# Conv-attention hybrid on one core: angles counted in turns on VectorE, centred weights, a new order table

## The chip, the core and the metric

The kernel runs on one core of one Trainium2 chip. The metric is device time in microseconds of that core, the median of several runs. Engines are named as the profile names them: PE is TensorE, PEld its weight load, DVE is VectorE, ACT is ScalarE, POOL is GpSimd, SP is SyncE.

## The reference

The input is x, 8 x 16 x 16 x 128 in float32: 8 batches of 256 tokens with 128 channels. Three layers follow one another; everything but the first softmax and the layer norms works token by token or head by head.

```
o  = gamma * softmax(f g^T) @ hh @ Wv + bv + xf     # f, g, hh: 16-wide projections of xf, with biases
t  = o
y  = LN(t)
c  = cos(y + theta); p = cumprod(c) per head, p[0] = prod(c[1:])     # 8 heads of 16
z  = y + softmax(p p^T / 4) p @ W_comb.T + b_comb
x1 = LN(z) * ln1_g + ln1_b
q  = cos(x1[:, :8]) * cos(phi)
z2 = x1 + relu(q @ W1.T + b1) @ W2.T + b2
t  = t + LN(z2) * ln2_g + ln2_b
u  = LN(t); sel = sigmoid(u @ expert_sel.T), the best 2 of 32 experts kept as weights w
t  = t + sum over experts of w * (relu(u @ keys) @ values)
```

LN subtracts the mean over the 128 channels and divides by the standard deviation. The biases and norm gains hold real numbers, not zeros and ones.

## The kernel before

One batch is two tiles of 128 tokens (`TB = 2`), kept with tokens on the partitions as 128 x 2 x 128. Every batch goes through six chains of steps, and there are 8 batches (`NB`):

- **conv**: x is transposed and projected by one weight matrix `wproj` (f, g and the product Wh Wv), f and g are split into three bf16 parts and stacked on POOL (`FGp`), scores, exp (`EA`), transposed (`ETs`), and multiplied with `HW` into `conv_ps`. DVE writes `T0 = conv_ps * gden + XR` (L854), where `gden` (L847) is gamma over the softmax sum and `XR` is x plus a constant row.
- **proj**: layer norm of T0 (`bn_stats` L765, `bn_aggr` L769 on DVE; `rsqrt` as two instructions on POOL, L1063 and L1065; `Y` on DVE, L775), then the angle Y + theta + pi/2, brought into a range that the Sin table takes, then Sin, cumulated products (L894), `PA`, and the fp16 parts `LS` and `RS`.
- **attn**: transposes of LS and RS, copied by DVE to `LT` (L907) and `RT` (L912), 8 score matmuls (L509) with 8 exps (L707), context (L519), a turn, the combination with `wcT_sb` (L542), `Z` (L925).
- **ffn**: layer norm of Z with its gain and bias (`ffn_norm`), 8 cosines per token, hidden layer, output (L570), `Z2` (L958).
- **norm**: second layer norm into `T1`, third into `XTK` (L775).
- **moe**: selection of experts, 4 pairs of matmul groups (L621, L625, and L606 into `moe_ps`), and `OB = moe_ps + T1` (L1013), which SP stores.

The angle's range is reduced in six instructions. POOL's `proj_angle` adds theta (L1135), and its helper `reduce_angle` finds the nearest number of whole turns by adding and taking away a large constant (L1070, L1072); then it makes `YB = Y + b_comb` (L1141), which `attn_combine` adds later. DVE's `proj_reduce` takes the turns off in two steps (L877, L880) and clamps (L885). The ffn chain does the same on 128 x 16 elements: POOL L1173, L1070, L1072, then `X1B` (L1177), DVE L939, L942, L947. `norm_affine` on DVE makes X1 in two passes, (Z - mean) * gain into `ZN` (L783) while POOL makes rstd, then times rstd plus bias (L788).

Each engine has one stream of instructions and takes them in order. `run_steps` sorts all 344 steps (name, batch) by one number and calls, on each engine, that engine's part of every step in that order; an engine whose part waits for a semaphore stands there, with everything behind it. Before, the number is a start of the step in its chain plus a start of the chain for the batch:

```
for _, b, name in sorted((at + CHAIN[name.split("_")[0]][b], b, name)
                         for name, at in START.items() for b in range(NB)):
```

The first conv output is followed by weight transposes on PE, and DVE's `proj_norm` of batch 0 ends with two small setup instructions (L863, L865). ACT loads a table of functions whenever the next function is in another set than the last one: Exp, Sin.

Of the kernel before, what the change touches and what calls it, by code (L numbers as in the profile page):

```python
# [26 lines left out]

START = {  # L30
    "conv_transpose": 0.000, "conv_project": 0.131, "conv_stack": 0.478, "conv_scores": 0.664, "conv_turn": 0.991,
    "conv_output": 1.190,
    "proj_norm": 0.000, "proj_angle": 0.375, "proj_reduce": 0.557, "proj_cos": 0.794, "proj_split": 1.014,
# [11 lines left out]
CHAIN = {
    "conv": (0.000, 4.654, 5.883, 7.128, 8.599, 9.969, 11.330, 12.652),
    "proj": (4.213, 6.104, 7.449, 8.826, 10.191, 11.562, 12.928, 14.505),
    "attn": (5.828, 7.430, 8.902, 10.276, 11.607, 12.925, 14.284, 15.872),  # L50
    "ffn": (7.444, 8.943, 10.284, 11.705, 13.063, 14.512, 16.131, 17.455),
    "norm": (9.557, 10.883, 12.224, 14.018, 15.617, 16.569, 18.277, 19.630),
    "moe": (10.535, 11.888, 13.236, 14.828, 16.048, 17.547, 18.900, 20.600),
# [1188 lines left out]
```

## Time and profile before

| | us |
|---|---|
| median of 3 runs | 266.65 (266.59 to 267.42) |
| span of the profiled execution | 265.1 |
| PE busy | 193.9 (73%) |
| DVE busy | 174.5 (66%) |
| ACT busy | 132.0 (50%) |
| POOL busy | 126.3 (48%) |

The span reaches from the first to the last instruction of one profiled execution. Of that execution's own time the profile gives only this span; the runs' times hold some 1.5 us more (266.65 less 265.1), which lie around it. Busy shares are averages over the whole span.

### The profile page before, as it was taken

The numbers are of one execution on the slowest core, as the hardware profiler recorded it, in microseconds if no ns is written. First come the engines' busy times: TensorE is split into PE (matmuls) and PEld (weight loads), VectorE is DVE, ScalarE is ACT, GpSimd is POOL, SyncE is SP. The second block draws the span as 40 slices with busy tenths as digits, with TensorE's granted clock in tenths as the row PEclk, the third lists the DMA queues.
The fourth block names the chain that finished last, engine by engine and source line by source line (L and its number), as shares of the span: only waits on it lengthen the run. The fifth ranks groups of instructions, "written<-read, shape, count | busy, mean of one in ns | idle before, by whom it ended". The sixth has DMA issues, their size and how long they took to land.

```text
span 265.1 us, 4762 instructions
## 1 busy us (share of the span) xinstructions
PE 193.9 (73%) x1488; PEld 144.9 (55%) x1488; DVE 174.5 (66%) x580; ACT 132.0 (50%) x276; POOL 126.3 (48%) x321
## 2 busy tenths in 40 slices
PE   3372466649775667998899889859788868597395
PEld 2161253423662445786488668637666747476265
DVE  1333464776858788977888788698767566347323
ACT  2523537457458166646846673855447362412021
POOL 3706798265757568555744743376153161022100
PEclk9999999995979979999999999999999999979869
DMA  3385000000000000000000000000000000000000
GB/s 64 107 162 117 0 1 4 0 1 2 0 0 2 0 1 4 0 2 21 1 2 0 22 0 1 22 0 4 0 22 2 1 19 2 21 0 0 22 0 20
DMA packets 12624, 4.33 MB, mean 16 GB/s; under 512 B 6276, under 2 KB 12472, under 8 KB 12600
## 3 DMA queue, kind: packets, MB, share of 16 engines
q1 hardware_dynamic: 12104, 3.94, 6.4%
q8 instruction: 12, 0.20, 0.3%
q10 hardware_dynamic: 496, 0.09, 0.2%
q14 instruction: 12, 0.10, 0.1%
HBM read 2.98 MB, written 1.05 MB: 15 GB/s over the span
## 4 chain that ended last, share of the span: by engine, by line
PE 38%; DVE 29%; issue 10%; POOL 10%; ACT 9%; DMA 1%; ACTq 1%; POOLq 0%; DVEq 0%
PE hidden_ps L621 9%; PE moe_ps L606 6%; PE ffn_ps L570 4%; POOL rstd L1065 4%; DVE HWT L1007 3%; DVE RT L912 3%; DVE st L765 2%; PE sc_ps L509 2%; PE attn_ps L519 2%; PE hidden_ps L625 2%; PE conv_ps L476 2%; PE conv_ps L441 2%; ACT EB_ L707 1%; DMA bv_b<-in_L_conv_bv 1%; DVE ARG L877 1%
## 5 line engine op out<-in xcount | busy, mean ns | idle before, releaser
L707 ACT ACTIVATE EB_<-sc_ps 128x512 f32<-128x512 f32 x64 | 35.1, 597 | 15.1 <-PE sc_ps L509 14.3
L621 PE MATMUL hidden_ps<-XTT,keys_sb 128*128 128x256 f32 x128 | 40.8, 412 | 2.4 <-DVE HWT L1007 2.4
L747 ACT ACTIVATE HR<-hidden_ps 128x256 f32<-128x256 f32 x64 | 24.4, 384 | 35.7 <-PE hidden_ps L625 35.5
L606 PE MATMUL moe_ps<-val_sb,HWT 128*128 128x128 f32 x256 | 33.9, 277 | 2.6 <-DVE HWT L1007 2.6
L606 PEld LDWEIGHTS moe_ps<-val_sb,HWT 128*128 128x128 f32 x256 | 31.0, 192 | 6.6 <-DVE HWT L1007 3.5
L1007 DVE TENSOR_TENSOR HWT<-hidden_ps,HR 128x256 f32<-128x256 f32 x64 | 25.1, 418 | 12.1 <-ACT HR L747 10.3
L1063 POOL TENSOR_SCALAR var<-mv 128x2 f32<-128x2 f32 x32 | 6.6, 205 | 53.2 <-DVE mv L769 52.7
L509 PE MATMUL sc_ps<-RT,LT 128*128 128x256 f16 x128 | 22.9, 290 | 10.0 <-ACT EB_ L707 4.6
L621 PEld LDWEIGHTS hidden_ps<-XTT,keys_sb 128*128 128x128 f32 x128 | 20.6, 202 | 9.3 <-DVE HWT L1007 4.6
L1065 POOL TENSOR_TENSOR rstd<-var,minushalf 128x2 f32<-128x2 f32 x32 | 22.3, 697 | 2.7
L509 PEld LDWEIGHTS sc_ps<-RT,LT 128*128 128x128 f16 x128 | 10.7, 102 | 19.8 <-issue 13.6
L519 PE MATMUL attn_ps<-EB_,PA 128*32 128x256 f32 x256 | 18.1, 403 | 3.2 <-ACT EB_ L707 3.1
L570 PE MATMUL ffn_ps<-w2T_sb,HID 128*128 128x128 f32 x128 | 18.5, 306 | 2.3 <-ACT HID L730 2.3
L570 PEld LDWEIGHTS ffn_ps<-w2T_sb,HID 128*128 128x128 f32 x128 | 17.5, 219 | 3.0 <-ACT HID L730 2.9
L625 PE MATMUL hidden_ps<-WT,spread 96*128 96x256 f16 x64 | 18.1, 283 | 0.8 <-DVE WT L998 0.8
L730 ACT ACTIVATE HID<-ffn_ps 128x512 f32<-128x512 f32 x16 | 9.6, 598 | 8.9 <-PE ffn_ps L563 8.9
L683 ACT ACTIVATE EA<-conv_ps,nmx 128x256 f32<-128x256 f32 x16 | 7.4, 470 | 9.8 <-DVE nmx L836 9.7
L519 PEld LDWEIGHTS attn_ps<-EB_,PA 128*32 128x32 f32 x256 | 6.9, 113 | 9.8 <-ACT EB_ L707 5.6
L912 DVE COPY RT<-sc_ps 64x1024 f16<-64x1024 f16 x16 | 11.1, 694 | 0.3
L775 DVE TENSOR_SCALAR XTK<-T,mv,rstd 128x128 f32<-128x128 f32 x16 | 4.9, 345 | 9.2 <-POOL rstd L1065 9.2
L673 ACT COPY HW<-conv_ps 128x256 f32<-128x256 f32 x8 | 3.0, 372 | 16.0 <-DVE FGs L824 16.0
L476 PE MATMUL conv_ps<-HW,ETs 128*128 128x128 f32 x64 | 9.8, 300 | 1.4 <-DVE ETs L843 1.4
(174 smaller groups left out, 449.0 us busy)
## 6 DMA issues: line engine op xcount, KB each, us to landing
X<-in_x SPq DMA_DIRECT2D x8, 128.0 KB, 7.9
out<-OB SPq DMA_DIRECT2D x8, 128.0 KB, 1.8
keys_sb<-in_L_ffn_keys SPq DMA_DIRECT2D x1, 512.0 KB, 7.8
val_sb<-in_L_ffn_values SPq DMA_DIRECT2D x1, 512.0 KB, 9.0
w_sb<-in_L_attn_W SPq DMA_DIRECT2D x1, 256.0 KB, 2.8
g_b<-in_L_attn_ln_g SPq DMA_DIRECT2D x2, 64.0 KB, 5.5
be_b<-in_L_attn_ln_b SPq DMA_DIRECT2D x2, 64.0 KB, 6.5
bv_b<-in_L_conv_bv ACTq DMA_DIRECT2D x1, 64.0 KB, 3.6
```

Of the source, the lines that this page charges most:

```text
L476: last = mm(conv_ps[:, t * C:(t + 1) * C], ETs[:, b % 2, m, t * P:(t + 1) * P], HW[:, b % 2, m, :], start=(m == 0), stop=(m == TB - 1))
L509: last = mm(sc_ps[h % 2][:, t * N:(t + 1) * N], LT[:, h // 2, t * P:(t + 1) * P], RT[:, h % 2, h // 2, :], start=True, stop=True)
L519: last = mm(attn_ps[32 * j:32 * j + 32, g * N:(g + 1) * N], PA[:, b % 2, t, h, :], EB_[:, h, t, :], start=(t == 0), stop=(t == TB - 1))
L570: last = mm(ffn_ps[:, t * C:(t + 1) * C], HID[:, k, t * P:(t + 1) * P], w2T_sb[:, k, :], start=(k == 0), stop=(k == FB - 1))
L606: last = mm(moe_ps[:, t * C:(t + 1) * C], HWT[:, k % 4, t * P:(t + 1) * P], val_sb[:, k, :], start=(k == 0 and t == 0), stop=(k == EB - 1) ...
L621: mm(hidden_ps[i][:, 0:N], keys_sb[:, k * EPB:(k + 1) * EPB, :].rearrange("p e h -> p (e h)"), XTT[:, b % 2, :], start=True, stop=True)
L625: mm(hidden_ps[i][:, N:2 * N], spread[:, k, :], WT[:, b % 2, :], start=True, stop=True).then_inc(s_moe_ps, 1)
L707: fn(EB_[:, h, :, :].rearrange("p t n -> p (t n)"), sc_ps[h % 2][:, :], ACT.Exp, scale=1.0 / math.sqrt(DK)).then_inc(s_prob, 1)
L747: fn(HR[:, k % 4, :], hidden_ps[i][:, 0:N], ACT.Relu).then_inc(s_relu, 1)
L912: V.tensor_copy(RT[q, i, :, :].rearrange("p j n -> p (j n)"), b16(sc_ps[0], F16)[q, :]).then_inc(s_RT, 1)
L1007: V.tensor_tensor(HWT[:, k % 4, :], hidden_ps[i][:, N:2 * N], HR[:, k % 4, :], ALU.mult).then_inc(s_hw, 1)
L1065: G.tensor_tensor(rstd[:, which, b, :], var[:, which, b, :], minushalf[:, :], ALU.pow).then_inc(rs, 1)
```

## The change

What the diff does, part by part:

- **Turns.** `reduce_angle` and POOL's part of it are gone. DVE's `proj_reduce` now has all three steps: turns = Y/(2 pi) + (theta/(2 pi) + 1/4), the nearest whole number by adding `ROUND`, and the fraction, which ACT's Sin takes with scale -2 pi. `ffn_angle` does the same on 16 columns. Nothing is clamped. `ARG` and `QA` shrink from 6 parts to 3.
- **Centred weights.** At setup DVE takes from b_comb its mean and from each row of the transposed W_comb its mean (`center`, three instructions each), so that Z less its mean needs no subtraction. `ffn_norm` on DVE is then one pass, Z * rstd * gain; `ZN` is gone. ln1_b no longer enters X1: it is added with b2 (`b12_b`) on POOL, and for the 8 angle columns in `be1q_b`.
- **Gamma** goes into `wproj` when it is copied from PSUM, which now waits for `w_in`; `gden` is gone.
- **Order.** `START` and `CHAIN` are replaced by one table of ranks, of which two rows stand below.

```diff
-START = {
+ORDER = {
...
+    "attn_transpose": (15, 45, 80, 114, 154, 191, 235, 273),
...
+    "ffn_norm": (54, 74, 118, 160, 188, 223, 282, 304),
...
             dve.wait_ge(s_wv_ps, 1)
-            V.tensor_copy(wproj[:, 2 * D:2 * D + C], hidden_ps[1][:, 0:C]).then_inc(s_wproj_sb, 1)
             dve.wait_ge(w_in, W_LOADED)
+            V.tensor_scalar(wproj[:, 2 * D:2 * D + C], hidden_ps[1][:, 0:C], gam[:, 0:1], None, ALU.mult).then_inc(s_wproj_sb, 1)
...
-                dve.wait_ge(s_crden, b + 1)
-                V.tensor_scalar(gden[:, b, :], rden[:, b, :], gam[:, 0:1], None, ALU.mult).then_inc(s_cgain, 1)
...
+            def center(dst, src, mean, summed, done):
+
+                V.tensor_reduce(mean[:, 0:1], src[:, :], AX.X, ALU.add).then_inc(summed, 1)
+                dve.wait_ge(summed, 1)
+                V.tensor_scalar(mean[:, 1:2], mean[:, 0:1], 1.0 / C, None, ALU.mult).then_inc(summed, 1)
+                dve.wait_ge(summed, 2)
+                V.tensor_scalar(dst[:, :], src[:, :], mean[:, 1:2], None, ALU.subtract).then_inc(done, 1)
...
-                    V.tensor_scalar(theta2[:, :], theta_b[:, :], math.pi / 2, None, ALU.add).then_inc(s_theta2, 1)
+                    V.tensor_scalar(theta2[:, :], theta_b[:, :], TURN, 0.25, ALU.mult, ALU.add).then_inc(s_theta2, 1)
+                    V.tensor_scalar(be1q_b[:, :], be1_b[:, 0:NQ], TURN, 0.25, ALU.mult, ALU.add).then_inc(s_be1q, 1)
+                    V.tensor_tensor(b12_b[:, :], be1_b[:, :], b2_b[:, :], ALU.add).then_inc(s_b12, 1)
+                    center(bcc_b, bc_b, bc_mean, s_bc_mean, s_bc)
+                    dve.wait_ge(s_wcT, 1)
+                    center(wcT_sb, wc_raw, wc_mean, s_wc_mean, s_wc)
...
             def proj_reduce(b):
-                dve.wait_ge(s_y_k, b + 1)
...
+                V.scalar_tensor_tensor(out=A[:, 0].rearrange("p t (h d) -> p (t h) d", d=DK),
+                                       in0=Y[:, b % 2].rearrange("p t (h d) -> p (t h) d", d=DK), scalar=TURN,
+                                       in1=theta2[:, None, :].to_broadcast([P, TB * H, DK]),
+                                       op0=ALU.mult, op1=ALU.add).then_inc(s_y_turns, 1)
+                dve.wait_ge(s_y_turns, b + 1)
+                V.tensor_scalar(A[:, 1], A[:, 0], ROUND, None, ALU.add).then_inc(s_y_near, 1)
+                dve.wait_ge(s_y_near, b + 1)
...
+                V.scalar_tensor_tensor(out=A[:, 2], in0=A[:, 1], scalar=ROUND, in1=A[:, 0],
+                                       op0=ALU.subtract, op1=ALU.subtract).then_inc(s_y_frac, 1)
...
-                norm_affine(b, X1[:, b % 2], ZN[:, b % 2], Z[:, b % 2], 1, s_z_mv, s_z_rstd, g1_b[:, :],
-                            [be1_b[:, :]] * TB, s_z_n, s_x1)
+                dve.wait_ge(s_z_rstd, b + 1)
+                for t in range(TB):
+                    last = V.scalar_tensor_tensor(out=X1[:, b % 2, t, :], in0=Z[:, b % 2, t, :], scalar=rstd[:, 1, b, t:t + 1],
+                                                  in1=g1_b[:, :], op0=ALU.mult, op1=ALU.mult)
+                last.then_inc(s_x1, 1)
...
-            def reduce_angle(b, A, a, k1, k):
...
-                G.tensor_tensor(ARG[:, b % 2, 0].rearrange("p t (h d) -> p (t h) d", d=DK),
...
-                reduce_angle(b, ARG[:, b % 2], s_y_arg, s_y_k1, s_y_k)
```

How the order moves, at the three places that the prediction speaks of. The first is DVE in the end of batch 0's `proj_norm` and its angle. Before (L865 is theta, L824 is batch 1's projection with its bias, L894 the cumulated product):

```order
L865 TENSOR_SCALAR theta<-theta_b 128x16
L775 TENSOR_SCALAR Y<-T,mv,rstd 128x128 x2
L877 SCALAR_TENSOR_TENSOR ARG<-ARG 128x256
L880 SCALAR_TENSOR_TENSOR ARG<-ARG 128x256
L885 TENSOR_SCALAR ARG<-ARG 128x256
L824 TENSOR_TENSOR FGs<-conv_ps,bfg 128x64
L894 SCALAR_TENSOR_TENSOR SC<-scanmask,CS 128x256
```

Now:

```order
L891 TENSOR_SCALAR theta<-theta_b 128x16
L892 TENSOR_SCALAR be1q_b<-be_b 128x8
L893 TENSOR_TENSOR b_b<-be_b,b_b 128x128
L878 TENSOR_REDUCE bc_mean<-bc_b 128x1
L880 TENSOR_SCALAR bc_mean<-bc_mean 128x1
L882 TENSOR_SCALAR bcc_b<-bc_b,bc_mean 128x128
L878 TENSOR_REDUCE wc_mean<-wc_raw 128x1
L880 TENSOR_SCALAR wc_mean<-wc_mean 128x1
L882 TENSOR_SCALAR wcT_sb<-wc_raw,wc_mean 128x128
L844 TENSOR_TENSOR FGs<-conv_ps,bfg 128x64
L795 TENSOR_SCALAR Y<-T,mv,rstd 128x128 x2
L909 SCALAR_TENSOR_TENSOR ARG<-Y,theta 128x256
L914 TENSOR_SCALAR ARG<-ARG 128x256
L918 SCALAR_TENSOR_TENSOR ARG<-ARG 128x256
L928 SCALAR_TENSOR_TENSOR SC<-scanmask,CS 128x256
```

Eight setup rows stand ahead of Y, and batch 1's projection (now L844) has moved from behind the angle's three rows to ahead of Y.

The second is PE from batch 1's conv scores on. Before (L492 and L499 are batch 0's attention transposes, L468 and L476 the turn and output of batch 1's conv, L432 the transpose of batch 2's x, L509 batch 0's attention scores):

```order
L468 MATMUL conv_ps<-ident,EA 128x128 x4
L492 MATMUL attn_ps<-identh,LS 128x128 x8
L499 MATMUL sc_ps<-identh,RS 128x128 x8
L476 MATMUL conv_ps<-HW,ETs 128x128 x4
L432 MATMUL conv_ps<-ident,X 128x128 x2
L509 MATMUL sc_ps<-RT,LT 128x256 x4
```

Now:

```order
L478 MATMUL conv_ps<-FGT 128x256 x2
L510 MATMUL attn_ps<-identh,LS 128x128 x8
L517 MATMUL sc_ps<-identh,RS 128x128 x8
L486 MATMUL conv_ps<-ident,EA 128x128 x4
L527 MATMUL sc_ps<-RT,LT 128x256 x8
L494 MATMUL conv_ps<-HW,ETs 128x128 x4
L537 MATMUL attn_ps<-EB_,PA 32x256 x8
L450 MATMUL conv_ps<-ident,X 128x128 x2
```

Batch 0's attention transposes have moved ahead of batch 1's turn, and the first four heads' scores (8 matmuls, L527) ahead of batch 1's conv output.

The third is DVE around batch 1's Z. Before (L925 is Z, L907 and L912 are the copies for batch 2's scores, L783 and L788 X1 of batch 1):

```order
L925 TENSOR_TENSOR Z<-attn_ps,YB 128x256
L824 TENSOR_TENSOR FGs<-conv_ps,bfg 128x64
L765 BN_STATS st<-T 128x6 x2
L769 BN_AGGR mv<-st 128x2 x2
L907 COPY LT<-attn_ps 128x1024
L912 COPY RT<-sc_ps 64x1024 x2
L765 BN_STATS st<-Z 128x6 x2
L769 BN_AGGR mv<-st 128x2 x2
L783 SCALAR_TENSOR_TENSOR ZN<-Z,mv,g_b 128x128 x2
L788 SCALAR_TENSOR_TENSOR X<-ZN,rstd,be_b 128x128 x2
```

Now:

```order
L959 TENSOR_TENSOR Z<-attn_ps,YB 128x256
L785 BN_STATS st<-Z 128x6 x2
L789 BN_AGGR mv<-st 128x2 x2
L968 SCALAR_TENSOR_TENSOR X<-Z,rstd,g_b 128x128 x2
L977 SCALAR_TENSOR_TENSOR QA<-X,be1q_b 128x16
L981 TENSOR_SCALAR QA<-QA 128x16
L985 SCALAR_TENSOR_TENSOR QA<-QA 128x16
L844 TENSOR_TENSOR FGs<-conv_ps,bfg 128x64
L941 COPY LT<-attn_ps 128x1024
L946 COPY RT<-sc_ps 64x1024 x2
```

`ffn_norm` and the ffn angle of batch 1 have moved ahead of the copies LT and RT (L941, L946) of batch 2. Batches 4, 5 and 7 have `ffn_norm` right behind Z too. On ACT the table loads in the whole program are 19, where they were 23.

## Rows read from the trace of the kernel before

**Rows 1.** Page, part 1: busy time of each engine.

```profile
PE 193.9 (73%) x1488; PEld 144.9 (55%) x1488; DVE 174.5 (66%) x580; ACT 132.0 (50%) x276; POOL 126.3 (48%) x321
```

**Rows 2.** Windows view: start:end, length, busy PE, PEld, DVE, ACT, POOL, granted clock.

```profile
60.00:120.00 60.00, 46.40 (x384) 33.56 (x379) 47.33 (x150) 34.82 (x74) 37.66 (x92) 0.90 0.01 1
120.00:190.00 70.00, 60.79 (x531) 47.44 (x532) 58.30 (x198) 43.53 (x93) 36.52 (x89) 1.00 0.02 7
190.00:245.00 55.00, 43.20 (x306) 33.28 (x304) 33.62 (x133) 24.11 (x51) 17.15 (x46) 0.97 0.03 8
```

**Rows 3.** Timeline of DVE: batch 7's Z; OB, batches 4, 7 (start, us, engine, line).

```profile
207.72 0.41 DVE L925 TENSOR_TENSOR Z<-attn_ps,YB 128x256 f32<-128x256 f32 x1
...
210.70 0.42 DVE L1013 TENSOR_TENSOR OB<-moe_ps,T 128x256 f32<-128x256 f32 x1 [0.95 <-PE moe_ps L606]
...
262.37 0.42 DVE L1013 TENSOR_TENSOR OB<-moe_ps,T 128x256 f32<-128x256 f32 x1 [0.94 <-PE moe_ps L606]
```

**Rows 4.** Timeline at the start: wproj copied, the first projection.

```profile
4.80 0.29 DVE L798 COPY wproj<-hidden_ps 128x128 f32<-128x128 f32 x1 [0.88 <-PE hidden_ps L408]
...
6.38 1.41 PE L441 MATMUL conv_ps<-wproj,XT 128*128 128x160 f32 x4 [1.00 <-DMA bv_b<-in_L_conv_bv]
```

**Rows 5.** Timeline, batch 0's angle and batch 1's projection, 19 to 27 us.

```profile
19.71 0.17 DVE L865 TENSOR_SCALAR theta<-theta_b 128x16 f32<-128x16 f32 x1
...
20.57 0.60 DVE L775 TENSOR_SCALAR Y<-T,mv,rstd 128x128 f32<-128x128 f32 x2 [0.70 <-POOL rstd L1065]
...
20.68 1.43 PE L441 MATMUL conv_ps<-wproj,XT 128*128 128x160 f32 x4 [0.46 <-ACT XT L666]
...
21.26 0.72 POOL L1135 TENSOR_TENSOR ARG<-Y,theta 128x256 f32<-128x256 f32 x1 [0.72 <-DVE Y L775]
...
22.92 0.72 POOL L1141 TENSOR_TENSOR YB<-Y,bc_b 128x256 f32<-128x256 f32 x1
...
22.99 0.94 DVE L877 SCALAR_TENSOR_TENSOR ARG<-ARG 128x256 f32<-128x256 f32 x1 [1.81 <-POOL ARG L1072]
...
24.42 0.29 DVE L885 TENSOR_SCALAR ARG<-ARG 128x256 f32<-128x256 f32 x1
...
24.63 0.22 DVE L824 TENSOR_TENSOR FGs<-conv_ps,bfg 128x64 f32<-128x64 f32 x1
...
25.27 1.28 ACT L691 ACT_TABLE_LOAD   x1
...
26.56 0.42 ACT L691 ACTIVATE CS<-ARG 128x256 f32<-128x256 f32 x1
```

**Rows 6.** Timeline, batch 0's first scores and batch 1's conv output, 33 to 38 us.

```profile
33.59 1.75 DVE L847 TENSOR_SCALAR gden<-rden,gam 128x2 f32<-128x2 f32 x1
...
33.66 0.94 POOL L1047 MEMSET spread<- 96x1024 f16 x1
...
34.49 1.61 DVE L912 COPY RT<-sc_ps 64x1024 f16<-64x1024 f16 x2
...
37.14 0.60 PE L509 MATMUL sc_ps<-RT,LT 128*128 128x256 f16 x4
```

**Rows 7.** Waits: who waited for whom, total us, times, longest.

```profile
DVE ARG L877 <- POOL ARG L1072: 5.0, 4, 1.8
...
DVE X L788 <- POOL rstd L1065: 3.8, 8, 0.9
...
DVE XTK L775 <- POOL rstd L1065: 9.2, 8, 1.2
```

**Rows 8.** Groups by line: count, busy us, mean ns; the last column is idle before.

```profile
L783 DVE SCALAR_TENSOR_TENSOR ZN<-Z,mv,g_b 128x128 f32<-128x128 f32 x16 | 4.9, 349 | 0.9
...
L724 ACT ACT_TABLE_LOAD x8 | 10.3, 1283 | 0.1
```

**Rows 9.** Instructions of one line: duration ns, minimum, median and maximum.

```profile
L877 DVE SCALAR_TENSOR_TENSOR ARG<-ARG x8: 418/736/937, 23.0 to 177.6; 128x256 f32<-128x256 f32 x8
...
L847 DVE TENSOR_SCALAR gden<-rden,gam x8: 228/228/1747, 16.0 to 155.7; 128x2 f32<-128x2 f32 x8
```

More of the change, by code:

```diff
@@ L47 @@
[L47 to L53, printed above, removed]
+ORDER = {
+    "conv_transpose": (0, 7, 24, 42, 76, 107, 136, 189),
+    "conv_project": (1, 8, 27, 43, 79, 110, 139, 190),
+    "conv_stack": (2, 12, 32, 46, 88, 115, 147, 210),
+    "conv_scores": (3, 14, 33, 48, 96, 116, 150, 213),
+    "conv_turn": (4, 16, 36, 53, 100, 121, 157, 217),
+    "conv_output": (5, 21, 39, 56, 103, 128, 181, 226),
+    "proj_norm": (6, 22, 44, 57, 104, 135, 185, 234),
+    "proj_angle": (9, 29, 51, 64, 113, 153, 200, 254),
+    "proj_reduce": (10, 34, 52, 70, 144, 171, 216, 263),
+    "proj_cos": (11, 37, 65, 83, 146, 176, 225, 265),
+    "proj_split": (13, 40, 72, 102, 149, 184, 229, 268),
+    "attn_transpose": (15, 45, 80, 114, 154, 191, 235, 273),
[10 rows of a table added]
+    "attn_turn": (35, 67, 101, 140, 182, 214, 258, 294),
+    "attn_back": (38, 71, 105, 143, 186, 219, 262, 298),
+    "attn_combine": (41, 73, 108, 151, 187, 222, 266, 300),
+    "ffn_norm": (54, 74, 118, 160, 188, 223, 282, 304),
+    "ffn_angle": (58, 75, 129, 170, 202, 231, 288, 305),
+    "ffn_cos": (68, 84, 134, 173, 218, 232, 295, 306),
+    "ffn_transpose": (69, 97, 141, 193, 227, 255, 301, 315),
+    "ffn_hidden0": (77, 109, 156, 209, 233, 259, 302, 318),
+    "ffn_hidden1": (78, 112, 168, 221, 236, 270, 303, 325),
+    "ffn_output": (81, 120, 174, 224, 241, 279, 308, 326),
+    "norm_second": (82, 126, 175, 237, 247, 293, 309, 330),
+    "norm_third": (93, 131, 198, 240, 271, 297, 319, 332),
+    "moe_transpose": (99, 155, 203, 250, 274, 310, 322, 335),
+    "moe_select": (106, 158, 206, 252, 275, 311, 323, 336),
+    "moe_topk": (111, 159, 212, 253, 278, 312, 324, 337),
+    "moe_spread": (130, 169, 215, 260, 285, 313, 327, 338),
[4 rows of a table added]
+    "moe_output": (152, 199, 245, 272, 307, 321, 334, 343),
@@ L113, in build @@
         s_theta2 = sem("s_theta2")
+        s_wc_mean = sem("s_wc_mean")
+        s_wc = sem("s_wc")
+        s_bc_mean = sem("s_bc_mean")
+        s_bc = sem("s_bc")
+        s_b12 = sem("s_b12")
+        s_be1q = sem("s_be1q")
         s_xT_ps = sem("s_xT_ps")
@@ L132, in build @@
         s_crden = sem("s_crden")
-        s_cgain = sem("s_cgain")
         s_t0 = sem("s_t0")
@@ L387, in run_steps @@
         def run_steps(steps):
-            for _, b, name in sorted((at + CHAIN[name.split("_")[0]][b], b, name)
-                                     for name, at in START.items() for b in range(NB)):
+            for _, b, name in sorted((at, b, name) for name, row in ORDER.items() for b, at in enumerate(row)):
                 step = name.rstrip("0123456789")
@@ L653, in turn_weights @@
                 act.wait_ge(s_wcT_ps, 1)
-                copy(wcT_sb[:, :], attn_ps[:, 0:P]).then_inc(s_wcT, 1)
+                copy(wc_raw[:, :], attn_ps[:, 0:P]).then_inc(s_wcT, 1)
                 act.wait_ge(s_w2T_ps, 1)
```

108 lines of the change are left out of this document (42 added, 66 removed), and 17 rows, old and new, of tables (ORDER, START).

## Prediction

> **What bounds the kernel now.** I read the busy shares first. No engine is full over the span: PE 73%, DVE 66%, ACT 50%, POOL 48% [rows 1]. The windows view tells the stages apart. From 60 to 120 us DVE is busy 47.33 of 60 us and PE 46.40; from 120 to 190 us DVE 58.30 of 70 and PE 60.79, that is 83% and 87% at a full granted clock; from 190 to 245 us DVE falls to 33.62 of 55 (61%) while PE stays at 79% [rows 2]. DVE also stands in waits that nothing can fill, since it takes its stream in order: 9.2 us for rstd ahead of XTK, 3.8 us ahead of X1 [rows 7]. So in the middle DVE and PE are both close to their limit, and what DVE no longer does there is worth nearly its whole duration. The end is another stage: batch 7's Z comes at 207.72, OB of batch 4 at 210.70 and of batch 7 at 262.37, so each of the last three batches takes 17.2 us after attention has stopped [rows 3]. The change removes nothing from the moe steps that fill this tail. I therefore count what it does to the 207.7 us ahead of it and carry that gain through unchanged. What is measured in busy shares is not what counts in the first 40 us: that is one chain of waits, and there I read the timeline.
>
> **The change part by part.**
>
> *Start.* The copy of wproj ran at 4.80, beside transfers still under way; the projection began at 6.38, when the last weight had landed [rows 4]. The copy with gamma now waits for that same transfer, and the projection waits for the copy: 0.29 us and a handoff of some 0.06. **+0.35 us.**
>
> *Batch 0's angle.* Behind theta at 19.71 + 0.17 now stand eight setup rows: two small (0.17 each by the theta row), plus the small ones in `center`; the wide ones are priced by a 128 x 128 pass of 0.349 us [rows 5, 8]. That is 0.17 + 0.35 + 2 x (0.35 + 0.17 + 0.35) = 2.26 us, until 22.1. There the projection of batch 1 has just left PE (20.68 + 1.43 = 22.11) [rows 5], so its bias add (0.22) ends at 22.4 instead of 24.85. Y (0.60) then ends at 23.0, 1.8 us later than before. The three angle steps are 0.42 to 0.94 (the shortest and longest L877, rows 9), 0.29 (the clamp at 24.42) and 0.42 by L877's shortest again: 1.1 to 1.7 us, ending at 24.1 to 24.7, where the six steps ended at 24.71. So the angle itself gains at most half a microsecond. What gains is the table: its load stood behind ACT's copy of batch 1's projection, began at 25.27 and let the cosine start at 26.56 [rows 5]. That copy comes 2.4 us earlier, the load ends at about 24.1, and the cosine starts with the fraction, between 24.2 and 24.8. **-1.9 us** (bounds -1.8 and -2.4).
>
> *gden.* Batch 0's lay beside PE's output matmuls. Batch 1's took 1.75 us, stuck while POOL set constants (a memset of 0.94 began beside it at 33.66), and the copies of batch 0's RT came only after it [rows 6]. The other six took 0.228 [rows 9], on an engine at 83%. 1.75 + 6 x 0.23 = 3.1. Below, the copy behind it could get stuck in its place, which leaves 1.4. I take **-3.1**, since the copies read PSUM and were not what waited.
>
> *Batch 0's scores ahead of batch 1's conv output.* The scores began at 37.14, though the copies ended at 34.49 + 1.61 = 36.10 [rows 6]; with the new order on PE they follow the copies directly. That is 1.0 us; the copies themselves could move up to gden's place, another 0.9 us (34.49 less 33.59). **-1.0** (bounds -1.0 and -1.9), since gden's term holds most of that 0.9 already.
>
> *DVE waiting for POOL's angle steps.* 5.0 us in four waits, 1.81 of it batch 0's, counted above [rows 5, 7]. The other 3.2 disappear, since DVE makes the turns from its own Y. As DVE was 79% busy in that stretch [rows 2], other waits will take part of the room: half, **-1.6** (bounds 0 and -3.2).
>
> *Angle steps on DVE.* Three out, three in, at like widths: L877's form, 0.42 alone, 0.29 and 0.42. **0** in work.
>
> *POOL.* It loses what stood between 21.26 and 22.92, 1.66 us with handoffs [rows 5], 13 us of 126 in eight batches, and three narrow ones of each ffn. POOL is no bound after 60 us (37.66 of 60, 36.52 of 70) [rows 2], so its own time is worth 0. But DVE instructions stretch while POOL works in the same memory: L877 took 0.94 where it began 0.07 us behind YB, 0.418 at best, 0.736 in the median [rows 5, 9]. With a tenth of POOL's work gone I take **-0.8** off DVE (0 to -2.5, which is 8 x (0.736 - 0.418)). By the Trainium skill (SBUF — State Buffer, § SBUF: two separate sides) the pair of ports that DVE and POOL share is an exclusive lock for a whole instruction. That speaks against the change where DVE's turns and POOL's YB are both released by the same Y; it is a rival below.
>
> *ZN.* 4.9 us of DVE work leave [rows 8]. They ran while POOL made rstd. XTK, which has nothing to do there, waits 9.2 us in 8 batches, X1 with ZN 3.8 [rows 7]; X1 without ZN will wait 9.2. 4.9 less 5.4: **+0.5**, in spite of the busy share that falls by 2%.
>
> *Setup beyond batch 0, b12 and be1q*: counted above. *X1B, YB*: the same instructions with other operands, 0.
>
> *Tables.* Four loads fewer on ACT. A load costs 1.283 us [rows 8] and its switch 1.29, from 25.27 to 26.56 [rows 5]: 5.1 us of an engine at 50%. About one in four of them lay where a score or cosine waited for ACT: **-1.3** (0 to -5.1). The Trainium skill (ScalarE: Activation LUTs, § What ACT_TABLE_LOAD costs) counts a drain of 1.38 us on top, 2.66 per switch; by it the four would be 10.6 us, estimated from that page, and this term -2.7. The trace has no such drain.
>
> Sum: 0.35 - 1.9 - 3.1 - 1.0 - 1.6 - 0.8 + 0.5 - 1.3 = **-8.8 us**. On the span that is 265.1 - 8.8 = 256.3; the runs' median lies 1.55 above the span, so **257.8 us** for the median of the runs. All terms at their weak ends give 0.35 - 1.8 - 1.4 - 1.0 + 0.5 = -3.35, so 263.3; all at their strong ends 0.35 - 2.4 - 3.1 - 1.9 - 3.2 - 2.5 + 0.5 - 5.1 = -17.35, so 249.3. The strong ends of waits that overlap do not add, and I let this case end at 253.
>
> **The rivals.** *The new order gives more.* DVE idles 12 of 70 us between 120 and 190 [rows 2]. The new table was not priced there at all. If it fills a third of it (3.9) and a third of the 12.7 from 60 to 120 (4.2), 8.1 more go: 249.7. For it: `norm` and `ffn` of batch 0 now stand together early. Against it: PE is at 87%, and only 9 us can go before it is full.
>
> *The lock takes the gain back.* YB is released by the same Y as the turns, and X1B by the same X1 as the ffn turns. If each of the 16 loses 0.52 us (0.94 - 0.42) [rows 5, 9] on top, that is 8.3 us and the time is 266.1, no change. For it: 22.92 and 22.99, where that happened. Against it: it happened already before (the median 0.736 holds it), and in six batches the new order puts other rows between Y and the turns.
>
> *`ffn_norm` stands in front of the scores.* Slower. In batches 1, 4, 5 and 7 DVE now makes batch b's X1 and its ffn angle right behind Z, ahead of LT and RT of batch b + 1, for which PE's scores and ACT's exps wait. Price: statistics and X1 each as long as Y (0.60), the unfilled wait 1.15 (9.2 / 8), three narrow angle steps like theta's (0.17) [rows 5, 7]: 2.9 us each. In batches 1, 4 and 5 a next batch's copies stand behind it, and every exp of that batch comes later: 8.7 us. With the terms for tables and POOL's waits failing too, since they are won on just these engines (2.9), the time is 257.8 + 8.7 + 2.9 = 269.4. It decides from the point where PE has less than 2.9 us of other work there. Against it: ffn hidden and output matmuls stand in PE's stream at these places, and the X1 that comes earlier lets moe start earlier.
>
> *The change does not do what it says.* POOL's angle steps could stay, or ACT's loads; the order of the changed program has neither the steps nor the four loads. No chance of its own.
>
> **How the numbers follow.** Forecast 257.8, own range 253 to 263: 0.57. More gain, 247 to 253: 0.14. Lock or otherwise used up: 0.15, of which 0.07 lies between 263 and 265.8 and 0.08 at no change. Slower: 0.14. A measurement here can tell 0.3% (0.8 us) from no change. Faster by more than that is 0.57 + 0.14 + 0.07 = 0.78, same 0.08, slower 0.14. The range that holds 8 in 10 cuts a third of the upper gain and nearly all of the slower case: 249.5 to 266.5.
>
> **What would show it.** The first projection at 6.7; batch 0's cosine near 24.6, its scores near 32 to 34; no DVE wait for POOL ahead of the turns; X1 waiting 9 us in 8 for rstd, as XTK does; gden's 1.75 gone and nothing of that length in its place; 19 table loads; Z of batch 7 near 199 and 54 to 55 us from there to the end. If Z of batch 7 is at 199 and the tail has grown, the tail is not the constant that I take it for; if the turns take 0.94 in the median, the lock was right; if LT of batches 2, 5 and 6 starts over 3 us behind Z with PE idle, the third rival was.

## The result, and the profile after

The changed kernel is slower, where the prediction said 257.8 us and faster: **270.38 us** in the median of 13 runs (268.71 to 272.30), the kernel before beside it 266.61. The ratio is **1.0129, 95% interval 1.0100 to 1.0158**, some 3.4 us. In all that follows the ratio to the kernel before decides, since disturbed runs are left out of it, while the medians in microseconds count every run and single executions of one kernel differ by several microseconds.

The span of the profiled execution is 270.1 us (265.1 before). Busy shares and TensorE's clock on the page of the profile after, for [rows 1]; the PEclk row has the granted clock in 40 slices of the span, in tenths of full speed:

```profile
PE 200.9 (74%) x1488; PEld 153.0 (57%) x1488; DVE 166.0 (61%) x564; ACT 127.1 (47%) x272; POOL 110.9 (41%) x273
...
PEclk9999996868689979999999999999799777979769
```

DVE has lost 8.5 us of work, POOL 15.4, ACT 4.9, as the diff says. PE has the same 1488 matmuls as before and is busy 7.0 us longer; its mean granted clock over the span is 0.912, where it was 0.955. The windows view after, with the columns and stretches of [rows 2]:

```profile
60.00:120.00 60.00, 47.79 (x401) 36.31 (x400) 43.33 (x142) 33.26 (x73) 32.66 (x78) 0.89 0.01 3
120.00:190.00 70.00, 59.52 (x509) 45.31 (x508) 52.88 (x186) 40.69 (x86) 30.15 (x71) 1.00 0.02 5
190.00:245.00 55.00, 42.62 (x276) 34.26 (x277) 29.72 (x112) 21.00 (x45) 13.34 (x34) 0.84 0.03 8
```

From 120 to 190 us DVE went from 58.30 to 52.88 busy and PE from 60.79 to 59.52: the room that DVE left was not filled. From 190 to 245 the granted clock is 0.84 where it was 0.97. DVE's timeline after, for [rows 3]: Z of batch 7 and OB of batches 4 and 7 (start, us, engine, line):

```profile
210.63 0.42 DVE L959 TENSOR_TENSOR Z<-attn_ps,YB 128x256 f32<-128x256 f32 x1
...
214.65 0.42 DVE L1052 TENSOR_TENSOR OB<-moe_ps,T 128x256 f32<-128x256 f32 x1
...
267.37 0.42 DVE L1052 TENSOR_TENSOR OB<-moe_ps,T 128x256 f32<-128x256 f32 x1 [0.95 <-PE moe_ps L626]
```

Z of batch 7 comes 2.9 us later than before, not 8.7 earlier, and from there to the last OB it is 56.7 us instead of 54.7. Yet the first local steps did what was said. The start and batch 0's angle after, for [rows 4, 5]:

```profile
6.43 0.35 DVE L819 TENSOR_SCALAR wproj<-hidden_ps,gam 128x128 f32<-128x128 f32 x1 [2.50 <-DMA bv_b<-in_L_conv_bv]
...
6.92 1.40 PE L459 MATMUL conv_ps<-wproj,XT 128*128 128x160 f32 x4 [1.54 <-DVE wproj L819]
...
22.61 0.59 DVE L795 TENSOR_SCALAR Y<-T,mv,rstd 128x128 f32<-128x128 f32 x2
23.24 0.43 DVE L909 SCALAR_TENSOR_TENSOR ARG<-Y,theta 128x256 f32<-128x256 f32 x1
...
24.49 0.42 ACT L711 ACTIVATE CS<-ARG 128x256 f32<-128x256 f32 x1
```

The waits view after, for [rows 7]; the first two rows are what grew (ACT's exps waiting for the score matmuls were 14.3 us before, POOL waiting for the selection of experts 16.8):

```profile
POOL W L1228 <- DVE SR L1030: 29.6, 7, 6.4
ACT EB_ L727 <- PE sc_ps L527: 24.8, 16, 4.0
...
DVE X L968 <- POOL rstd L1104: 9.7, 8, 1.6
...
DVE XTK L795 <- POOL rstd L1104: 9.2, 8, 1.2
```

No wait of DVE for POOL is left ahead of the turns. Their durations after, for [rows 9] (minimum, median, maximum):

```profile
L909 DVE SCALAR_TENSOR_TENSOR ARG<-Y,theta x8: 411/418/627, 23.2 to 180.8; 128x256 f32<-128x256 f32 x8
```

### The profile page after: what moved, and what is told of

Its sections match the earlier page's. It is cut to its first block, busy times and chain, and to the rows that moved or that the text cites. A ratio compares the mean times of both kernels' runs of the same rounds, so it can differ in the third digit from the quotient of the medians.

```text
span 270.1 us, 4683 instructions
## 1 busy us (share of the span) xinstructions
PE 200.9 (74%) x1488; PEld 153.0 (57%) x1488; DVE 166.0 (61%) x564; ACT 127.1 (47%) x272; POOL 110.9 (41%) x273
## 4 chain that ended last, share of the span: by engine, by line
PE 45%; DVE 19%; POOL 11%; ACT 11%; issue 10%; DMA 1%; ACTq 1%; POOLq 0%; DVEq 0%
PE hidden_ps L641 9%; PE moe_ps L626 7%; PE ffn_ps L590 6%; PE attn_ps L537 4%; PE conv_ps L494 3%; ACT EB_ L727 3%; PE sc_ps L527 3%; POOL rstd L1104 3%; PE hidden_ps L645 2%; PE conv_ps L459 2%; DVE HWT L1046 2%; DVE RT L946 2%; PE conv_ps L486 2%; ACT EA L703 2%; DVE st L785 2%
## 5 line engine op out<-in xcount | busy, mean ns | idle before, releaser
L626 PE MATMUL moe_ps<-val_sb,HWT 128*128 128x128 f32 x256 | 34.5, 279 | 1.5 <-DVE HWT L1046 1.5
L1046 DVE TENSOR_TENSOR HWT<-hidden_ps,HR 128x256 f32<-128x256 f32 x64 | 25.9, 421 | 15.2 <-ACT HR L767 13.0
L626 PEld LDWEIGHTS moe_ps<-val_sb,HWT 128*128 128x128 f32 x256 | 31.6, 194 | 4.8 <-DVE HWT L1046 1.9
L527 PE MATMUL sc_ps<-RT,LT 128*128 128x256 f16 x128 | 21.8, 279 | 6.6 <-ACT EB_ L727 3.9
L590 PE MATMUL ffn_ps<-w2T_sb,HID 128*128 128x128 f32 x128 | 21.1, 334 | 1.0 <-ACT HID L750 1.0
L590 PEld LDWEIGHTS ffn_ps<-w2T_sb,HID 128*128 128x128 f32 x128 | 20.3, 249 | 1.7 <-ACT HID L750 1.5
L527 PEld LDWEIGHTS sc_ps<-RT,LT 128*128 128x128 f16 x128 | 10.4, 99 | 14.9 <-issue 11.0
L1228 POOL TENSOR_TENSOR W<-SG,SR 128x64 f32<-128x64 f32 x8 | 2.6, 326 | 29.6 <-DVE SR L1030 29.6
L494 PE MATMUL conv_ps<-HW,ETs 128*128 128x128 f32 x64 | 11.7, 340 | 1.8 <-DVE ETs L863 1.8
L494 PEld LDWEIGHTS conv_ps<-HW,ETs 128*128 128x128 f32 x64 | 10.2, 242 | 3.8 <-DVE ETs L863 3.3
L795 DVE TENSOR_SCALAR XTK<-T,mv,rstd 128x128 f32<-128x128 f32 x16 | 5.9, 408 | 9.2 <-POOL rstd L1104 9.2
```

Source lines behind the costliest of these rows:

```text
L494: last = mm(conv_ps[:, t * C:(t + 1) * C], ETs[:, b % 2, m, t * P:(t + 1) * P], HW[:, b % 2, m, :], start=(m == 0), stop=(m == TB - 1))
L527: last = mm(sc_ps[h % 2][:, t * N:(t + 1) * N], LT[:, h // 2, t * P:(t + 1) * P], RT[:, h % 2, h // 2, :], start=True, stop=True)
L590: last = mm(ffn_ps[:, t * C:(t + 1) * C], HID[:, k, t * P:(t + 1) * P], w2T_sb[:, k, :], start=(k == 0), stop=(k == FB - 1))
L626: last = mm(moe_ps[:, t * C:(t + 1) * C], HWT[:, k % 4, t * P:(t + 1) * P], val_sb[:, k, :], start=(k == 0 and t == 0), stop=(k == EB - 1) ...
L1046: V.tensor_tensor(HWT[:, k % 4, :], hidden_ps[i][:, N:2 * N], HR[:, k % 4, :], ALU.mult).then_inc(s_hw, 1)
```

## The experiments

### Instructions or order

e1 has the changed instructions in the order of before, e2 the instructions of before in the new order.

```diff
# e1, from the changed kernel
-for _, b, name in sorted((at, b, name) for name, row in ORDER.items() for b, at in enumerate(row)):
+for _, b, name in sorted((at + CHAIN[name.split("_")[0]][b], b, name)
+                         for name, at in START.items() for b in range(NB)):
# e2, from the kernel before: the same lines the other way round
```

> The changed instructions (turns on VectorE, centred weights, gamma in wproj) in the order of steps of the kernel before. Order theory: the instructions gain, and the new table of ranks alone costs; then this is faster than before by 3 to 6 us (261 to 264 us). Instruction theory (longer unfilled waits for rstd, VectorE and GpSimd in each other's way at the turns): this is as slow as the changed kernel, 269 to 271 us.

> The instructions of before in the new order of steps. Order theory: slower than the changed kernel, 273 to 278 us, since it has the table's losses and none of the gains. Instruction theory: near before, 265 to 268 us.

Measured: e1 261.4 us, ratio **0.9809** (0.9768 to 0.9850). e2 278.9 us, ratio 1.0353 (1.0292 to 1.0415). So the instructions are worth -5 us and the new table costs +9, with either set of instructions (1.0129 less 0.9809 is 3.2%, 1.0353 less 1 is 3.5%): the two add up. On e1's timeline of DVE (the fastest of its six executions, 260.57 us) batch 7's Z and the last OB are

```profile
200.21 0.41 DVE L940 TENSOR_TENSOR Z<-attn_ps,YB 128x256 f32<-128x256 f32 x1
...
255.46 0.42 DVE L1033 TENSOR_TENSOR OB<-moe_ps,T 128x256 f32<-128x256 f32 x1 [0.94 <-PE moe_ps L607]
```

that is Z at 200.2, where the prediction had 199, and a tail of 55.3, where it had 54 to 55.

### Which instructions

e4 is the kernel before with gamma in `wproj` and `gden` gone. e9 is e1 without the centring.

```diff
# e4, from the kernel before
-V.tensor_copy(wproj[:, 2 * D:2 * D + C], hidden_ps[1][:, 0:C])
+V.tensor_scalar(wproj[:, 2 * D:2 * D + C], hidden_ps[1][:, 0:C], gam[:, 0:1], None, ALU.mult)
-V.tensor_scalar(gden[:, b, :], rden[:, b, :], gam[:, 0:1], None, ALU.mult)
# e9, from e1
-center(bcc_b, bc_b, bc_mean, s_bc_mean, s_bc)
-center(wcT_sb, wc_raw, wc_mean, s_wc_mean, s_wc)
-V.scalar_tensor_tensor(out=X1[...], in0=Z[...], scalar=rstd[...], in1=g1_b[:, :], ...)
+norm_affine(b, X1[:, b % 2], ZN[:, b % 2], Z[:, b % 2], 1, s_z_mv, s_z_rstd, g1_b[:, :], ...)
```

> Before, with gamma in the value projection and without gden, nothing else. By my sum: +0.35 at the start, -1.75 where gden of batch 1 was stuck, -1.4 for the other six: 263.8 us. If another VectorE instruction gets stuck in gden's place, or VectorE's time in the middle is worth less than its duration, it is 265.5 to 267 us.

> The new instructions in the old order gave 261.4 us, 5.5 less than before, and gamma alone gave nothing. Here the centring is undone as well (X1 in two passes again, the pool of mean and W_comb as before), so that turns and gamma are left. If the turns carry the gain (batch 0's angle, VectorE not waiting for POOL's angle steps, POOL relieved), about 261.5 to 262.5. If the centring carries it (one pass of X1 less on VectorE, 4.9 us of work in all), 265 or more.

Measured: e4 ratio **1.0002** (0.9968 to 1.0036): nothing. e9 263.84 us, ratio 0.9867 (0.9824 to 0.9909). The turns carry about 3.5 us. The centring carries the rest, 1.5 us against e1 and 2.6 against its repetition below; the intervals touch, so its sign is likely and its size is not settled. In e4 the long instruction is gone. The stretch of [rows 6] before, with the copy LT that started beside gden, and the same stretch in e4:

```profile
33.40 0.15 DVE L845 RECIPROCAL rden<-den 128x2 f32<-128x2 f32 x1
...
33.72 1.61 DVE L907 COPY LT<-attn_ps 128x1024 f16<-128x1024 f16 x1
...
36.14 0.61 DVE L854 SCALAR_TENSOR_TENSOR T<-conv_ps,gden,XR 128x128 f32<-128x128 f32 x2
```

```profile
33.99 0.15 DVE L845 RECIPROCAL rden<-den 128x2 f32<-128x2 f32 x1
34.24 0.69 DVE L905 COPY LT<-attn_ps 128x1024 f16<-128x1024 f16 x1
35.09 1.41 DVE L910 COPY RT<-sc_ps 64x1024 f16<-64x1024 f16 x2 [0.16 <-PE sc_ps L499]
36.68 0.61 DVE L852 SCALAR_TENSOR_TENSOR T<-conv_ps,rden,XR 128x128 f32<-128x128 f32 x2 [0.18 <-PE conv_ps L476]
```

Batch 1's T starts 2.69 us behind its reciprocal, where it was 2.74 before (36.14 less 33.40). The 1.75 us were never 1.75 us of DVE's stream: LT's record began 0.13 us behind gden's, and the copies were through 2.70 us behind the reciprocal. In e4 they are through at 2.51, and T then waits 0.18 us for PE.

### Where in the table

e5 tests the prediction's own slow rival, e3 the most visible wait of the profile after. e6, e7 and e8 take the first 100 or 200 steps from one table and the rest from the other.

```diff
# e5, steps in the order of the changed kernel
-ffn_norm[1] ffn_angle[1] ... attn_transpose[2]
+attn_transpose[2] ... ffn_norm[1] ffn_angle[1]
# and ffn_norm[4] behind attn_transpose[5]; ffn_norm, ffn_angle, ffn_cos [5] behind attn_transpose[6]
# e3
-ffn_hidden1[6] ... ffn_output[6] norm_second[6] moe_transpose[5] moe_select[5] moe_topk[5]
+... moe_transpose[5] moe_select[5] moe_topk[5] ffn_hidden1[6] ffn_output[6] norm_second[6]
# e6, e7: new[:100] or new[:200], then the others in the old order; e8: old[:200], then new
```

> The changed kernel with ffn_norm (and the angle steps behind it) of batches 1, 4 and 5 put back behind attn_transpose of the next batch, as it stood before. My third rival (the norm in front of the scores costs 2.9 us three times): 261 to 264 us. If the loss lies elsewhere in the table: 269 to 271 us.

> The changed kernel with three steps moved in the table: ffn_hidden1, ffn_output and norm_second of batch 6 go behind moe_topk of batch 5, so that TensorE has them to do while the experts of batch 5 are selected (in the changed kernel it waits 4.5 us there and then runs at half clock). Tail theory: 4 to 5 us faster than the changed kernel, 265 to 267 us. If the tail is only where an earlier delay shows, or if the matmuls moved only make the selection later, the gain is under 1.5 us, 269 to 270 us.

> Changed instructions; the first 100 of 344 steps in the new order, all others in the old order. If the loss of the table comes early (TensorE's clock granted at 0.73 to 0.76 between 40 and 80 us in the changed kernel): 266 to 269 us. If it comes later: 260 to 263 us, as with the old order throughout (261.4).

> Changed instructions; the first 200 steps in the new order, the others in the old order. If the middle of the table loses (Z of batch 3 comes 8.4 us later than with the old order): 267 to 270 us. If the loss is that of the last third (Z of batches 6 and 7 over 10 us late, a wait of 4.5 us in the selection of batch 5): 261 to 264 us.

> Changed instructions; the first 200 steps in the old order, the others in the new order. If the last third loses: 267 to 271 us. If the first two thirds lose: 260 to 263 us. If losses add up over the whole table, both this and the reverse lie between, 264 to 267 us.

Measured: e5 282.14 us, ratio **1.0543** (1.0493 to 1.0592): the placing of `ffn_norm` that the rival blamed is worth 11 us, in favour of the changed kernel. e3 274.2, ratio 1.0267 (1.0231 to 1.0303): also slower than the changed kernel. The wait that it was to fill is this one, on PE of the changed kernel, ahead of the transposed expert weights of batch 5:

```profile
217.83 0.63 PE L607 MATMUL moe_ps<-selT_sb,XTT 128*128 128x32 f32 x4 [0.46 <-ACT XTT L754]
222.96 0.45 PE L617 MATMUL moe_ps<-identh,WP 128*96 128x128 f16 x2 [4.50 <-POOL WP L1232]
223.21 1.17 PE L641 MATMUL hidden_ps<-XTT,keys_sb 128*128 128x256 f32 x2
```

e3 has no such wait: the weights are on PE at 221.12. But DVE copies them at 224.23 instead of 223.45, since the moved norm of batch 6 (its T at 223.70 instead of 219.52) now stands ahead of that copy and itself waited for PE. e6 265.38, ratio 0.9925 (0.9889 to 0.9961). e7 263.42, ratio 0.9868 (0.9811 to 0.9925). e8 268.58, ratio 1.0042 (1.0006 to 1.0079). Against e1's 0.9809 the first 100 steps cost 1.2%, the first 200 together 0.6%, the last 144 2.3%.

### The last 74 steps

e10 narrows it further, e17 and e18 split the last 74, e13 and e14 put two moves back in e10, e15 makes them in the changed kernel, e16 repeats e1 beside them.

```diff
# e10: old[:270], then new.  e17: old[:310], then new.  e18: new only for steps 270 to 309
# e13, from e10; e14 = e13 and the second pair of lines
-moe_pair3[3] ... norm_third[4] ... moe_select[4] attn_scores0[7] attn_scores1[7]
+moe_pair3[3] attn_scores0[7] attn_scores1[7] ... norm_third[4] ... moe_select[4]
-moe_select[4] moe_topk[4] ffn_output[5] attn_scores2[7] attn_scores3[7] ffn_norm[6]
+moe_select[4] ffn_norm[6] moe_topk[4] ffn_output[5] attn_scores2[7] attn_scores3[7]
# e15: the changed kernel with the moves of e14, attn_transpose[7] ahead of the scores. e16: e1
```

> Changed instructions, old order for the first 270 steps, new order for the last 74. Old throughout gave 261.4, old for the first 200 gave 268.6: some 7 us are lost behind step 200. Theory one: they are lost in the end, where the selection of experts of batch 5 has nothing of batch 6 beside it; then this kernel still takes 267 to 269. Theory two: they are lost between steps 200 and 270, where the new table puts the attention of batch 5 first and the one of batch 6 late (28.9 us from one Z to the next, 18.4 in the old order); then it takes 261.5 to 263.5.

> Old order for 270 steps, new for the last 74 (269.0 us), with one thing put back: the first two score steps of batch 7 stand again right behind the last pair of experts of batch 3, and not behind the selection of batch 4, for which TensorE stood idle 1.95 us with the scores ready behind it (first scores 7.5 us after the transposes instead of 2.5). Theory: this is the greater part, 265 to 266.5. Rival: those scores are hidden, since the exps and the pairs of experts are behind; then 268.5 to 269.

> As e13, with the norm of batch 6 also put back ahead of the selection's steps on VectorE (in the new order X1 of batch 6 comes 17.0 us behind its Z, in the old 12.3, and VectorE waits 2.48 us for ACT in between). Theory: both together give back 5 of the 7 us, about 263.5 to 264.5. If only the scores counted, as e13; if the loss is somewhere in the last 50 steps, 267 or more.

> The changed kernel (270.4 us) with the same two moves in its own order: transposes and first two scores of batch 7 ahead of the third norm and the selection of batch 4, the norm of batch 6 ahead of that selection's steps. If what e13 and e14 look for is a loss by order alone, it shows here too: 265.5 to 267. If it hangs on the order of the first 270 steps, 269.5 or more.

> The changed instructions in the old order, unchanged from e1 (261.4, ratio 0.9809), on the chip of e13 to e15. If e10's 7 us are the order's, 261 to 262 again. If the spread between chips is in it, 264 or more.

> Changed instructions, old order for 310 steps, new for the last 34 (they differ in the places of batch 6's and 7's output and norm steps among the pairs of batch 5). Old throughout gave 261.4 and 263.5 (ratios 0.981 and 0.977). If the loss is in steps 270 to 310, ratio 0.976 to 0.982, that is 261 to 262.5. If it is in the end, 0.99 or more.

> The complement: new order for steps 270 to 310 only, old before and behind. If the loss is there, ratio 1.00 to 1.007 as e10 and e13 (267 to 269). If in the last 34, 0.98. If both come out near 0.99, the loss is spread and not the work of one place.

| | us | ratio | 95% interval |
|---|---|---|---|
| e16 old order again | 263.53 | 0.9768 | 0.9707 to 0.9829 |
| e17 new in the last 34 | 265.56 | 0.9922 | 0.9885 to 0.9959 |
| e18 new in 270 to 309 | 269.48 | 1.0044 | 1.0001 to 1.0087 |
| e10 new in the last 74 | 268.98 | 1.0065 | 1.0028 to 1.0103 |
| e13 e10, scores put back | 268.51 | 1.0010 | 0.9969 to 1.0050 |
| e14 e13, norm put back | 266.52 | 0.9956 | 0.9916 to 0.9995 |
| e15 both in the changed kernel | 271.96 | 1.0153 | 1.0092 to 1.0214 |

e16 confirms e1. Forty steps, 270 to 309, in the new order cost 2.4% by themselves (e18 against e1), as much as the last 144 did. The last 34 alone cost 1.1%; the parts do not add. The two moves of e14 give back 1.1% of e10's 2.6 in all, less than the 5 of 7 us expected, and in the changed kernel nothing.

The most visible delay on the timelines is not where the loss is. Z of batch 5 comes at 155.57 in the changed kernel and at 156.06 in e1, Z of batch 6 at 184.52 and 174.50: 28.95 us from one to the next instead of 18.44. With the old order up to step 270 (e10) it is 19.66 us, yet e10 (1.0065) is no faster than e8 (1.0042), which has steps 200 to 269 in the new order.

One reading of why the two moves did little comes from the traces one step further on. All of these kernels but e15 have the same instructions in front of step 270. Taking executions that had been equally fast until then, Z of batch 6 stands at 174.5 in e1, 175.3 in e13 and in e18; from there to the last OB it is 81.0, 86.9 and 86.4 us, and from Z of batch 6 to Z of batch 7 already 25.7, 29.8 and 30.2. e12 (the old order at this place, below) and e14, both with Z of batch 6 at 176.2, have 27.1 and 29.7 there. That is batch 7's attention. PE in e1, where scores 2 and 3 stand ahead of batch 5's ffn output (L571):

```profile
186.39 0.38 PE L508 MATMUL sc_ps<-RT,LT 128*128 128x256 f16 x2
186.61 1.95 PE L571 MATMUL ffn_ps<-w2T_sb,HID 128*128 128x128 f32 x16
188.49 1.07 PE L518 MATMUL attn_ps<-EB_,PA 128*32 128x256 f32 x16
```

PE in e14, where that output (L590, 16 matmuls in fp32) still stands ahead of them:

```profile
186.68 0.44 PE L601 MATMUL moe_ps<-ident,XTK 128*128 128x128 f32 x2 [1.83 <-DVE OB L1052]
187.58 0.63 PE L607 MATMUL moe_ps<-selT_sb,XTT 128*128 128x32 f32 x4 [0.46 <-ACT XTT L754]
188.04 3.36 PE L590 MATMUL ffn_ps<-w2T_sb,HID 128*128 128x128 f32 x16
191.19 0.96 PE L527 MATMUL sc_ps<-RT,LT 128*128 128x256 f16 x4
193.00 1.07 PE L537 MATMUL attn_ps<-EB_,PA 128*32 128x256 f32 x16 [0.85 <-ACT EB_ L727]
```

and ACT, which makes the exps, in e14 and then in e1:

```profile
188.25 0.22 ACT L758 ACTIVATE SE<-moe_ps 128x64 f32<-128x64 f32 x1 [0.72 <-PE moe_ps L607]
191.86 1.09 ACT L727 ACTIVATE EB_<-sc_ps 128x512 f32<-128x512 f32 x2 [3.39 <-PE sc_ps L527]
```

```profile
189.92 2.24 ACT L708 ACTIVATE EB_<-sc_ps 128x512 f32<-128x512 f32 x4 [2.45 <-PE sc_ps L508]
```

ACT stands idle for 3.39 us in e14, and the output takes 3.36 instead of 1.95 us at a granted clock of 0.58 from 188 to 191 us, behind waits of 1.83 and 0.46 us (1.00 from 183 to 186). The changed kernel has the same place (3.25 us at 193.08, ACT idle 2.61 us until 196.59).

This is a reading, not a shown cause. In e1 the same output stands ahead of the next four scores, and ACT waits 2.45 us behind it (4.0 us in e16, a longer execution of the same program, where it ran partly at the lower clock); and the changed kernel needs only 26.1 us from Z of batch 6 to Z of batch 7, hardly more than e1. A kernel with scores 2 and 3 ahead of that output was not run.

### The clock

e11 is the changed kernel, e12 is e1, with matmuls that nobody reads in the waits for the expert weights.

```diff
 def moe_spread(b):
+    if b in (5, 7):                 # e12: b == 7, 12 times
...
+        for _ in range(14):
+            mm(conv_ps[:, :], w1T_sb[:, 0:P], w1T_sb[:, 0:512], start=True, stop=True)
     pe.wait_ge(s_w_l, b + 1)
```

> The changed kernel with 14 matmuls of 512 columns, whose result nobody reads, ahead of the waits of 4.5 and 3.2 us for the experts' weights of batches 5 and 7. If the low clock behind such waits is part of the loss, the matmuls after them run at full clock (the ones of 1.17 and 1.06 us take 0.60) and the time falls by 2 to 3 us, to 267.5 to 268.5. If the clock is only a sign of waiting that lies elsewhere, the time stays at 270.4 within 0.5, or grows by the overhang of the added matmuls.

> The changed instructions in the old order (261.4) with 12 such matmuls ahead of batch 7's wait of 3.2 us alone. The last pairs of experts, some 8 matmuls at half clock behind that wait, are on the path to the end: if the clock is the cause, 1.2 to 1.8 us less, about 260. If not, 261.4 or a little more.

Measured: e11 271.06 us, ratio 1.0101 (1.0044 to 1.0158), against 1.0129 without them; e12 ratio 0.9743 (0.9688 to 0.9797), against 0.9809 and 0.9768. Neither can be told from no change. PE's timeline of e11 shows why this does not settle what the clock costs:

```profile
218.40 3.19 PE L616 MATMUL conv_ps<-w1T_sb 75*128 75x512 bf16 x14
223.06 0.31 PE L622 MATMUL moe_ps<-identh,WP 128*96 128x128 f16 x2 [1.47 <-POOL WP L1237]
223.21 1.09 PE L646 MATMUL hidden_ps<-XTT,keys_sb 128*128 128x256 f32 x2
...
253.85 6.03 PE L616 MATMUL conv_ps<-w1T_sb 75*128 75x512 bf16 x14
```

In the first gap they took 0.228 us each, at 2.4 GHz, and 1.47 us of idle time were left; the pair behind took 1.09 and not 0.60 all the same. In the second gap they took 0.431 each: PE was at 1.2 GHz (granted 0.50 from 254 to 260 us), and 6.03 us of them stood in a wait that had been 3.2; this execution was the longest of its six (275.28 us). So what the lower clock costs by itself stays open.

## Why the prediction was wrong

**The step that failed** is the one that costed the order at nothing: the sum has only gains for the table (batch 0's angle and scores, four table loads fewer) and nothing for what it does elsewhere, and where the rivals come to it, "The new table was not priced there at all". It costs 9 us (e1 against the changed kernel, e2 against before). The three order fences ahead of the prediction show two places that were priced as gains and one where `ffn_norm` moved; the steps 270 to 309, which cost 2.4% by themselves, were in none of them. Had batch 7's scores been followed through the new order, they would have been found behind a selection and an ffn output, on an engine at 79 to 87%. Which of the forty steps costs the time stays open: the two moves tried there gave back 1.1% of 2.6, and nothing in the changed kernel.

**The direction rested on a wrong idea of slack.** DVE's and PE's busy shares were read as nearness to a limit, so that work taken off DVE would count almost whole. e4 says otherwise: gden's work is gone and the time is the same. The terms that do not hang on the order (start, gden, POOL's waits, POOL, ZN) sum to -4.65 us, and e1 and e16 measured 5.1 and 6.2; that this half came out is partly luck, since gden's 3.1 were nothing and the centring gave where +0.5 was said. The other three (batch 0's angle and scores, tables), -4.2 us, stand against the +9. An argument that no run isolates: where PE is at 87%, a batch's next step finds PE taken, and the order decides who is served first.

Term by term, by e1, e4, e9 and the profile after:

- *Start*, +0.35: batch 0's T came at 18.59 for 18.05 before, +0.54. The copy of wproj ran 0.35, not 0.29.
- *Batch 0's angle*, -1.9: the cosine at 24.49, predicted 24.6, before 26.56. Right as a local step, but mostly the order's: in e1 it is at 25.98. By batch 0's Z nothing of it was left (next term but one).
- *gden*, -3.1: wrong. The 1.75 us instruction is gone and nothing as long took its place, but e4 is 1.0002. Its record had been counted as time of DVE's stream, while LT's and RT's records lay beside it; and the 0.228 us of the others were not on the path either.
- *Scores of batch 0*, -1.0: they began at 32.70 in place of 37.14, so the local step was larger than said. By batch 0's Z it was lost (49.97 against 49.59; e1, in the old order, 48.20). The granted clock fell there (1.00 from 40 to 42 us, 0.50 from 43 on; the turn of CT at 42.79 took 1.06 us for 0.66 before), but that is not the reason by itself: e6 has the same steps, its turn took 0.60, and its Z came at 50.74.
- *Waits for POOL's angle steps*, -1.6, *POOL*, -0.8: the waits are gone, the turns take 0.418 in the median (0.736 for L877 before), and e9 gives 3.5 us to the turns, batch 0's angle included, where the three terms have 4.3. Right within what e9 can tell. The bound of 2.5 took the median for the mean: before, four of the eight L877 took 0.94, the other four 0.42 to 0.54, 2.2 us in all.
- *ZN*, +0.5: X waits 9.7 us, predicted 9.2, but the sign is likely wrong: e1 is faster than e9 by 1.5 to 2.6 us. The wait did take the place of the pass (X1 waited 3.8 before); what of the centring then helps, no run separates.
- *Tables*, -1.3: 19 loads, as counted. What they were worth no run separates; e1 has all 23 and is 9 us faster, so the order that saved them cost more.
- *Tail*: 54 to 55 us as a constant. In e1 55.3, in the changed kernel 56.7, in e7 52.8, in e14 57.4. It depends on the order.

**The rivals.** *Lock*: right in its mechanism, wrong in its size. Before, YB began 0.07 us ahead of L877 in four batches, and each of these L877 took 0.94 us. Now YB and the turns begin together in one batch only, DVE first:

```profile
56.51 0.42 DVE L909 SCALAR_TENSOR_TENSOR ARG<-Y,theta 128x256 f32<-128x256 f32 x1
56.55 0.96 POOL L1166 TENSOR_TENSOR YB<-Y,bcc_b 128x256 f32<-128x256 f32 x1 [1.00 <-DVE Y L795]
56.96 0.70 DVE L914 TENSOR_SCALAR ARG<-ARG 128x256 f32<-128x256 f32 x1
```

DVE's turns took their 0.42 us, POOL's YB 0.96 instead of 0.73, and then DVE's second step, begun while YB ran, 0.70 instead of 0.29. The second ffn step (L981) stretched likewise in four batches, 0.59 to 0.72 for 0.17. Together that is 2.2 us, where the rival had 8.3. The Trainium skill (SBUF — State Buffer, § SBUF: two separate sides) has VectorE and GpSimd exclude each other for whole instructions in some forms, whichever starts first; these rows agree. *`ffn_norm` in front of the scores*: the time came out within 1 us of its 269.4, by luck: e5 refutes the reason. *The new order gives more*: the opposite. The slower side had a chance of 0.14, and the range ended at 266.5.

## What to carry to other kernels

Where every engine takes its stream in order, a new order is a change like any other and must be followed, batch by batch, at the engine that is waited for: here it cost 9 us and the instructions gave 5 to 6. Test it apart first, with the old instructions in the new order and the reverse. Do not trust the largest new wait on the page, or the latest step on a timeline: filling the wait (e3) made things worse, since the steps moved into it stood ahead of awaited ones on another engine, and undoing the 29 us between two Z (e10 against e8) gained nothing. A long fp32 product in front of short matmuls that another engine waits for is a place to look at, not one that was shown to be the loss. The kernel to keep is e1, which takes all the changed instructions and leaves the order alone.
